# Attention and int4 feed-forward on one core: the scaling and splitting of the second tile's weights placed elsewhere in the first tile

## The reference, cut to what matters

```python
def _layernorm(x, axis=-1, eps=1e-05):
    m = jnp.mean(x, axis=axis, keepdims=True)
    v = jnp.var(x, axis=axis, keepdims=True)
    return (x - m) / jnp.sqrt(v + eps)

# cross attention (pcd_up = layernorm(x), pcd_down = the context)
q = jnp.einsum('oc,bcn->bon', Wq, pcd_up)
k = jnp.einsum('oc,bcm->bom', Wk, pcd_down)
v = jnp.einsum('oc,bcm->bom', Wv, pcd_down)
attention = jax.nn.softmax(jnp.einsum('bcn,bcm->bnm', q, k) / scale, axis=-1)
x = x + jnp.einsum('oc,bcn->bon', Wskip, pcd_up) + jnp.einsum('bnm,bcm->bcn', attention, v)

# feed-forward on layernorm(x); the weights are packed int4 with a scale and a zero per 64 inputs
w = (nibble - zero) * scale
h = jax.nn.silu(einsum('bsh,ih->bsi', x, Wg)) * einsum('bsh,ih->bsi', x, Wu)
x = x + einsum('bsi,hi->bsh', h, Wd)
```

## Time and profile before

| | us |
|---|---|
| median of 3 runs | 1407.02 |
| lowest and highest | 1406.82, 1407.9 |
| the profiled execution, device time | 1410.28 |
| its span | 1408.1 |
| PE busy | 1386.9 (98%) |
| DVE busy | 1117.1 (79%) |
| ACT busy | 689.6 (49%) |
| POOL busy | 310.2 (22%) |

### The profile page before, as it was taken

How to read it: one execution, slowest core, us unless ns; L and a number is a source line. 1 busy time by engine, 2 the same in 40 slices (tenths; PEclk the granted TensorE clock), 3 DMA queues, 4 the chain that set the end, 5 groups by cost and what they waited for, 6 DMA issues and landing times.

```text
span 1408.1 us, 19597 instructions
## 1 busy us (share of the span) xinstructions
PE 1386.9 (98%) x6414; PEld 677.3 (48%) x6414; DVE 1117.1 (79%) x1598; ACT 689.6 (49%) x1279; POOL 310.2 (22%) x365
## 2 busy tenths in 40 slices
PE   8999998999999999999999999999999999999999
PEld 6676764444444444444444444444444444444443
DVE  6888978887877877878778788788788788788376
ACT  6899984344344444344444444343444444444330
POOL 1132332122122122122222212212222212212200
PEclk9999999999999999999999999999999999999999
DMA  6222222286486576576576666756846746748596
GB/s 191 101 102 86 83 90 61 53 157 120 97 147 122 103 134 123 105 138 118 105 136 111 126 118 119 136 108 116 146 95 124 129 108 123 126 100 154 98 299 261
DMA packets 58982, 174.83 MB, mean 124 GB/s; under 512 B 8000, under 2 KB 11072, under 8 KB 54592
## 3 DMA queue, kind: packets, MB, share of 16 engines
q0 software_dynamic: 34560, 83.90, 38.4%
q1 hardware_dynamic: 24096, 90.20, 20.9%
q10 hardware_dynamic: 288, 0.26, 0.1%
HBM read 73.67 MB, written 100.66 MB: 124 GB/s over the span
## 4 chain that ended last, share of the span: by engine, by line
PE 91%; DVE 4%; ACT 2%; issue 2%; POOL 0%; DMA 0%; SPq 0%; DVEq 0%; POOLq 0%; ACTq 0%
PE ps L590 52%; PE ps L628 9%; PE ps L629 9%; PE ps L630 9%; PE ps L553 3%; PE ps L523 2%; PE ps L793 2%; PE ps L511 2%; PE ps L752 1%; PE ps L548 1%; PE ps L542 1%; ACT temps L859 1%; ACT temps L833 1%; DVE stats L1263 0%; DVE neg_max L1294 0%
## 5 line engine op out<-in xcount | busy, mean ns | idle before, releaser
L590 PE MATMUL ps<-xt,w_gu 128*128 128x512 f16 x3528 | 796.1, 379 | 5.7 <-DVE temps L1510 1.7
L590 PEld LDWEIGHTS ps<-xt,w_gu 128*128 128x128 f16 x3528 | 344.8, 98 | 422.7 <-ACT temps L939 2.6
L972 ACT ACTIVATE stage<-ps,pow 128x512 f32<-128x512 f32 x300 | 204.3, 687 | 323.6 <-PE ps L630 317.6
L1540 DVE SCALAR_TENSOR_TENSOR stage<-ps,pow,stage 128x512 f32<-128x512 f32 x220 | 160.1, 747 | 106.1 <-ACT stage L972 67.2
L628 PE MATMUL ps<-park 128*128 128x512 f16 x560 | 212.9, 380 | 2.0 <-ACT stage L972 2.0
L629 PE MATMUL ps<-park 128*128 128x512 f16 x560 | 213.0, 380 | 0.0
L630 PE MATMUL ps<-park 128*128 128x512 f16 x560 | 212.9, 380 | 0.0
L437 POOL DMA_DIRECT2D out<-stage x80 | 70.6, 883 | 429.0 <-DVE stage L1540 429.0
L451 POOL DMA_DIRECT2D out<-stage x80 | 69.2, 865 | 296.4 <-ACT stage L972 296.4
L969 ACT CAST park<-temps 128x512 f16<-128x512 f32 x140 | 83.2, 615 | 64.8 <-DVE temps L1524 38.1
L1537 DVE TENSOR_TENSOR park<-temps,park 128x512 bf16<-128x512 f32 x140 | 98.3, 708 | 17.0 <-ACT park L969 14.0
(11 more groups left out here) (137 smaller groups left out, 1623.4 us busy)
## 6 DMA issues: line engine op xcount, KB each, us to landing
out<-stage POOLq DMA_DIRECT2D x80, 512.0 KB, 5.3
out<-stage POOLq DMA_DIRECT2D x140, 256.0 KB, 5.3
grid<-grids SPq DMA_DIRECT2D x136, 256.0 KB, 6.1
raw<-packed SPq DMA_DIRECT2D x34, 512.0 KB, 4.2
out<-stage SPq DMA_DIRECT2D x16, 512.0 KB, 2.6
stage<-x SPq DMA_DIRECT2D x12, 512.0 KB, 3.6
xt<-out SPq DMA_DIRECT2D x12, 512.0 KB, 12.1
out<-xt SPq DMA_DIRECT2D x12, 512.0 KB, 2.6
```

The lines of the kernel that those rows point to most:

```text
L590: mm = pe.matmul(bank, w_gu[e][:, wp, w, P * j:P * j + P], xt[:, xb, xp, j, cols], start=(fresh and n == 0), stop=(n == 3 * J - 1), skip_g ...
L972: return act.activation(dst, ps[:, bank, :], ACT.Copy, scale=pow2[:, 10:11])
L1540: return dve.scalar_tensor_tensor(out=part, in0=ps[:, bank, :], scalar=pow2[:, 10:11], in1=part, op0=ALU.mult, op1=ALU.add)
```

## The change

Only two functions change, both called `first_tile`; nothing is added or removed, and TensorE's and GpSimd's own lists stay as they are.

```diff
@@ ScalarE, first_tile
                 if 1 <= at < 5:
                     block_hi(LATE[at - 1])
                     sum_hi(*((LAST - 1, T1), (LAST - 1, T2), (LAST - 1, T4), (LAST, T3))[at - 1])
-                if at == 2:
+                if at == 1:
                     plain_hi(2, 1)
                 if at == 4:
                     mixed_hi(4, 1, 0)
@@ VectorE, first_tile
                 if at == 1:
                     row_stats(1, B - 1)
+                    times_scale(q, 3, 6)
                     normalize(1, B - 1)
+                    times_scale(r, 4, 6)
                     block_done(LATE[0])
-                if at == 2:
-                    job_scale(1, 6)
                 if at in (3, 4):
                     block_done(LATE[at - 1])
+                if at == 2:
+                    plain_lo(1, 4)
                 if at == 3:
-                    plain_lo(1, 4)
+                    first_sums(4, 4)
                 if at == 4:
-                    first_sums(4, 4)
                     second_sums(4)
                 if at == 5:
                     mixed_lo(1, 4)
```

## The result

| | median us | executions | ratio to before |
|---|---|---|---|
| before | 1407.8 | 14 | |
| changed | 1410.55 | 14 | 1.0023, 95% interval 1.0016 to 1.003 |

The medians differ by 2.75 us, 0.20%; the ratio as estimated with its interval is 1.0023, which is 3.2 us, between 2.3 and 4.2 us. The forecast was 2.6 us. Of the three signs, slower by over 0.2% came true by the ratio; it had 0.30, and "same" had 0.68. By the difference of the medians the result lies just at the border of 2.8 us, so the sign was close either way.

The account below looks back on a forecast made before the run. TensorE is busy nearly throughout, but VectorE's order was taken to pace the changed stretch. `c12_out` 1.2 us late plus 1.4 for the clock gave 1407.02 + 2.6 = 1409.6 us; range 1406.9 to 1411.2.

Parts of the forecast that it names:

- three signs: Whole kernel: slower (from 1409.8 us) had chance 0.30, same 0.68, faster 0.02; about 0.2%, 2.8 us, is the measurable difference.
- late block late by: VectorE's `LATE[0]`: its low part ends at 225.10 instead of 222.03, 3.07 us late.
- wait ahead of `LATE[1]`: TensorE, after its fourth product, waits from 220.93 to 225.25 for `LATE[0]`'s low part: 4.3 us, not 1.24.
- wait ahead of the seventh product: TensorE's wait for `c22_out` becomes 1.4 us instead of 1.67.
- `c12_out` late, without the clock: VectorE's `c12_out` at 239.98 instead of 238.75, 1.2 us late, carried unchanged to the end.
- part 1: Scaling of q ahead of the normalisation: GpSimd's addition takes 1.06 us for 0.19, so `rstd` comes 0.90 us late.
- part 2: Scaling of r ahead of the late block: waits for GpSimd's second L407, ends at 223.90; late block 3.07 us late.
- part 3: Low parts ahead of `u2_out` cost nothing; two sums move ahead of `c22_out`: it comes 2.66 us late, `c12_out` 1.2.
- part 4: ScalarE's copy of `LATE[1]`, held up by r, ends at 227.5, needed at 228.4: 0.9 us of cover, no cost.
- part 5: TensorE's clock falls to half behind the 4.3 us wait; costs 0 to 1.7 us, taken as 1.4.
- the row's 1.70: Earlier trace near 1329.26, behind a 1.98 us TensorE wait: 12 matmuls took 4.29 us for 2.59, costing 1.70.
- fourth rival: Clock stays low or falls again at TensorE's seventh product: 4.6 us over before, 1411.6 us; chance 0.15.

Follow-up runs that it names:

- e4: Changed kernel plus 16 matmuls into an unread PSUM bank between TensorE's fourth product and the transposes of `LATE[1]`; 1408.42 us, ratio 1.0009.
- e10: The changed kernel run again without an edit, for one more profile; this execution took 1411.27 us at a mean clock of 0.998.
- e3: Changed kernel with GpSimd alone waiting, ahead of its last eight low parts of sums, until both scalings are done; 1408.08 us, ratio 1.0004.
- e6: Against e1, the first two sums also back in gap 4, so only the low parts stay moved; 1407.15 us, ratio 0.9998.
- e7: Against e2, 8 more matmuls into an unread PSUM bank in TensorE's wait for `LATE[0]`; 1408.05 us, ratio 1.0005.
- e1: Changed kernel with both scalings back behind the late block, ScalarE's high parts back in gap 2, low parts behind `u2_out`, sums still moved; 1405.81 us.
- e5: Against e1, the late block `LATE[0]` moved ahead of the last row's normalisation; 1405.18 us, ratio 0.9986.
- e2: Changed kernel with the scaling of r behind the late block instead of ahead of it; 1408.08 us, ratio 1.001.
- e8: Against e5, both scalings behind `u2_out`, q's low part ahead of `LATE[2]`, r's behind it, a ScalarE copy one gap later; 1407.61 us.

## Why the prediction was right, and where its sizes were off

The path forecast is the path measured, step by step:

| step | forecast | measured |
|---|---|---|
| addition on GpSimd behind the statistics | 1.1 | 1.05 |
| `rstd` late by | 0.90 | 0.86 |
| scaling of r takes | 2.3 | 2.17 |
| late block late by | 3.07 | 2.95 |
| wait ahead of `LATE[1]` | 4.3 | 4.19 |
| wait ahead of the seventh product | 1.4 | 1.25 |
| `c22_out` late, without the clock | 2.66 | 2.52 |
| `c12_out` late, without the clock | 1.2 | 1.08 to 1.10 |
| the clock | 1.4 | 1.67 (e4), 2.6 where the stretch was long (e10) |
| whole | 2.6 | 2.75 |

"Late" is against before, each counted from the aggregate; without the clock means less the 4.44 - 2.75 = 1.69 us by which the slow product is longer (1.10 is e4's). That the whole comes out at 2.75 for 2.6 is in part luck: the terms before the clock came out 0.1 too high, the clock's 0.3 too low, and the interval of the measurement, 2.3 to 4.2 us, is wider than either error.

- **q in the gap** (part 1): right. The gap was not VectorE's own: GpSimd needed it. Part of the 1.00 us idle was filled, 0.71 stayed, and `rstd` came late.
- **r** (part 2): right, GpSimd had asked first (the second L407 was issued at 220.28, r at 220.79) and had its turn first. e3 shows the cause without touching VectorE's order.
- **Low parts and sums** (part 3): the arithmetic held for the two moves together, but the place of the sums, 1.43 out and 1.32 in and so priced at 0.1 us, is worth 1.14 (e6), since in the changed order the sums fill an idle time that the low parts' departure opens. The sum of the change hid this.
- **ScalarE's cover** (part 4): held. In e4, at the full clock, the copy of `LATE[1]` ended at 227.13 and TensorE came at 228.06: 0.93 us of cover for 0.9. With TensorE earlier, in e7, it was gone, a wait of 1.44 us.
- **The clock** (part 5): the mechanism was right and the size too small. I discounted the row's 1.70 to 1.4 for a stretch partly in the wait or in cover. In the first profile it lies wholly in the slow product, on the way, and costs its full 1.67 to 1.69; in e10 it costs 2.6, above the prediction's upper bound of 1.7. That is what brought the result to the border of 0.2%.
- **The fourth rival**, a second fall at the seventh product, did not occur in the three profiles of the changed kernel. The slower execution that was profiled, e10, has one longer stretch instead.
- **The profiled execution of before**: I put its 3.3 us over the median down to profiling. 2.3 us of it lie behind `c12_out`, 1.7 of them in the low stretch of the earlier trace rows. Profiled executions of the other kernels lie on both sides of their medians (e1 1405.59 for 1405.81, e4 1409.29 for 1408.42). I took the price of a fall from that row and didn't see that the same row explained the execution.

What stays open is how many of the seven executions at 0.998 or 0.997 have the long stretch, why it is long in one and not in another, and why the clock seems to fall behind waits of 2.1 to 2.5 us in some executions and not in others.

## What to carry to other kernels

An idle gap of one engine is free only if nobody else works in it on something that the filler blocks; ask what the awaited engine does in the gap, and look in the trace for the same pair of neighbours. Fill such a gap with work that shares nothing with the awaited engine, and put the rest where the engine idles for a third one. When a wait of TensorE grows, price the matmuls behind it at the lower clock too, but only as far as no other engine is late anyway. And when two moves are priced as one sum, ask what each would be worth without the other: here the sums filled an idle time that the low parts had opened.

## What the runs showed of the hardware

- A VectorE instruction with two SBUF inputs (or the 128x1024 normalisation) and a GpSimd instruction on SBUF excluded each other, with either of them as the one held up: 0.19 to 1.05 us for a 128x1 addition, 1.28 to 2.17 for a scaling, 0.81 to 1.63 for a normalisation. VectorE instructions that read PSUM and one SBUF input ran at 0.68 us beside GpSimd.
- In the changed kernel the one that was issued first went first: L407 (issued at 219.17), L1277 (219.24), the second L407 (220.28), L1391 (220.79); each of the last three was held until the one ahead of it had ended. In e5 it was otherwise by a hair: L1277 was issued at 219.13, GpSimd's second L407 at 219.17, both before the end of the first L407 (219.21, by the usual 1.16 us); the second ran 1.16 us, not held up, and L1277 waited for it (1.74 us).
- Where TensorE's longest wait in the stretch was 1.67 us or less, the mean clock was 1.000, with one exception in 66 executions of before and none in 43 of e1, e4, e5 and e7; with 2.1 to 2.5 us (e2, e3, e6, e8) it was lower in 25 of 44, and the profile of each of these four shows the fall right there; with 4.19 us it was lower in all 14.
- The wait near 1330 us is a second place for a fall, which the mean clock can't tell from the first: behind 1.98 us the clock fell (before), behind 1.94 (e10) and 1.79 (e4) it did not.
